# Constant matmuls in four of TensorE's waits, in the last two steps of a token loop

## Chip, cores and metric

The kernel runs on one core of one Trainium2 chip. The metric is the device time of one execution in microseconds (us). Engines are named as in the profile: PE is TensorE's matmul side, PEld its weight loads, DVE is VectorE, ACT is ScalarE, POOL is GpSimd, SP is SyncE.

## What is computed

The input x is 32 sequences of 64 tokens with 256 features, 2048 tokens in all. The reference, cut to its outline (every product in float32, except where the fake quantisation rounds):

```python
moe  = two_of_eight_experts(x, cond)              # three layers per expert, relu
x1   = x + tanh(softmax(causal(q k^T)) v @ Wo + bo)   # q, k, v = tanh(moe @ W + b), 16 heads of 64
a    = field_attention(x1, cond) @ Wout.T + bout      # 16 heads of 16, a coherence gate and a field term
x_q  = mxfp4_pseudo_quant(a, delta_act)           # blocks of 32 features
out  = x1 + x_q @ w_q.T + bias
```

## The kernel before

The kernel has three stages. A setup stage routes the tokens; an expert stage runs 39 slot tiles of 128 tokens; the last stage, called the token loop here, takes the 2048 tokens in TT = 16 tiles of 128. Each engine has its own program, written out by hand in the order in which it is to run, and semaphores tie the programs together. There is no scheduler: what stands later in an engine's program runs later on that engine.

The token loop is a software pipeline, `for t in range(0, TT + 3)`, so steps 0 to 18. In step t PE works on the first attention of tile t (names beginning `l1_`), finishes that of tile t-1, works on the second attention of tile t-2 (`l2_`), and on the last product of tile t-3 (`l2_turn_q`, `l2_ffn`). Every function first asks whether its tile exists and returns at once if not. So in steps 17 and 18 most of PE's program falls away:

- Step 17 (t = TT+1) has for PE the hidden layer and keys of tile 15 (L749, L737), its coherence gate (L758) and scores (`l2_scores`, L783), its values (`l2_v`, L768), then for tile 14 the transpose of the quantised rows (`l2_turn_q`, L823) and the last product (`l2_ffn`, L832), and then for tile 15 eight transposes (`l2_turn_p`, L685), the context (`l2_context`, L805) and the output projection (`l2_out`, L815).
- Step 18 (t = TT+2) has only `l2_turn_q` (L823) and `l2_ffn` (L832) of tile 15.

These wait for DVE or ACT. `l2_v` waits for the shifted scores (DVE L1398), because its result goes where the scores stood. `l2_turn_q` waits for the rounded rows (DVE L1079 to L1099), `l2_ffn` for the copy by ACT (L1044), `l2_turn_p` for the shares (DVE L1420). DVE then adds the field to the transposed shares (L1429, one for each half, the first as soon as four of the eight transposes are there), and PE's context (L805) waits for the second. After the context come the copy by ACT (L1038), the projection (L815), and on DVE the bias (L1436) and the blockwise rounding (L1079 to L1099). The last DVE instruction of a tile is `l2_result` (L1456), and SP stores what it wrote. A DVE program is strictly in order too: in step 17 `l2_result` of tile 14 stands between `l2_share` (L1420) and the first field addition of tile 15.

The waits of three of these functions in PE's program:

```python
def l2_v(t):       pe.wait_ge(u2_set, 2 * t + 2)
def l2_turn_q(t):  pe.wait_ge(xq_set, t + 1)
def l2_turn_p(t, n):                       # n == 0 / n == 1
    pe.wait_ge(p2_set, t + 1)  /  pe.wait_ge(fin_set, t)
```

PSUM bank 0 is used by the first attention only, whose last tile is read out in step 16. `ident_h` is a 128x128 identity matrix in bf16, held in the buffer `before` (the profile shows that name) since the expert stage. The f32 matmuls show twice as many instructions in the trace as the program has, the bf16 ones as many.

Of the kernel before, what the change touches and what calls it, by code (L numbers as in the profile page):

```python
# [26 lines left out]
P = 128  # L27
BATCH, SEQ, HID, COND = 32, 64, 256, 64
TOK = BATCH * SEQ
TT = TOK // P  # L30
# [46 lines left out]
def exists(t, n):  # L77

    return not isinstance(t, int) or 0 <= t < n
# [19 lines left out]
def build(nc, t_in, out):  # L99
    ctx = ExitStack()  # L100
    with ctx:
# [25 lines left out]
        ident_h = before  # L127
# [124 lines left out]
        bank = lambda b, n=512, parts=P: ps[0:parts, b, 0:n]  # L252
# [231 lines left out]
        def _(pe):  # L484
            mm = pe.matmul
# [4 lines left out]
            for k in range(KH):  # L490
                for g in range(4):
                    mm(ps[g * GATE_PAD:(g + 1) * GATE_PAD, 0, :], gate_w[:, k, :], x_t[:, k, g * 512:(g + 1) * 512],
                       start=k == 0, stop=False, tile_position=(0, g * GATE_PAD))
            pe.wait_ge(aug_loaded, 16)
            for g in range(4):
                mm(ps[g * GATE_PAD:(g + 1) * GATE_PAD, 1, :], gg_w,
                   part("cond", AUG_K)[:, g * 8:(g + 1) * 8].unsqueeze(2).to_broadcast([AUG_K, 8, SEQ]),
                   start=True, stop=True, tile_position=(0, g * GATE_PAD))
            for k in range(KH):
                pe.wait_ge(squared, k + 1)  # L500
                for g in range(4):
                    last = mm(ps[g * GATE_PAD:(g + 1) * GATE_PAD, 0, :], ones_w, sq_t[:, k, g * 512:(g + 1) * 512],
                              start=False, stop=k == KH - 1, tile_position=(0, g * GATE_PAD))
# [3 lines left out]
            for b, src in ((2, gate_t), (3, cond_t)):  # L507
                for n in range(4):
                    last = pe.transpose(ps[:, b, n * P:(n + 1) * P], src[:, n * P:(n + 1) * P], ident[:, :])
# [3 lines left out]
            for k in range(KH):  # L513
                last = mm(ps[:, 4, k * BATCH:(k + 1) * BATCH], part("we1", COND + 1)[:, k * P:(k + 1) * P],
                          part("cond", COND + 1), start=True, stop=True)
            for k in range(KH):
                last = mm(ps[:, 4, (KH + k) * BATCH:(KH + k + 1) * BATCH], part("wc1", AUG_K)[:, k * P:(k + 1) * P],
                          part("cond", AUG_K), start=True, stop=True)
# [7 lines left out]
            for n in range(TOPK * TT):  # L526
                last = mm(bank(0, 2 * SLOT_TILES), lo_hot[:, n, :], hi_ids[:, n, :, :], start=n == 0, stop=n == TOPK * TT - 1)
# [5 lines left out]
            for k in range(KH):  # L533
                last = mm(ps[0:BATCH, 7, 0:HID], f_hid[:, k, :], we2[:, k, :], start=k == 0, stop=k == KH - 1)
# [86 lines left out]
            def halves():  # L621

                return [(s, slice(s * SEQ, (s + 1) * SEQ)) for s in range(2)]

            def l1_turn_m(t):
                if not exists(t, TT):
                    return
                pe.wait_ge(m_set, t + 1)
                if t:
                    pe.wait_ge(exp1_set, 2 * t)  # L630
                for k in range(KH):
                    last = pe.transpose(ps[:, 0, k * P:(k + 1) * P], m_rows[:, k * P:(k + 1) * P], ident[:, :])
                last.then_inc(mt_ps, 1)

            def l1_project(t, wt, n):
                b = (3, 0)[n]
                for c in range(4):
                    f = (n * 4 + c) * P
                    for k in range(KH):
                        last = mm(ps[:, b, c * P:(c + 1) * P], wt[:, k, f:f + P], m_t[:, k, :],  # L640
                                  start=k == 0, stop=k == KH - 1)
                last.then_inc(qk_ps, 1)

            def l1_q(t, n):
                if not exists(t, TT):
                    return
                if n == 0:
                    pe.wait_ge(mt_set, t + 1)
                l1_project(t, wq, n)

            def l1_k(t, n):
                if not exists(t, TT):
                    return
                pe.wait_ge(qk_set, 4 * t + n + 1)
                l1_project(t, wk, n)

            def l1_v(t, s):
                if not exists(t, TT):
                    return
                pe.wait_ge(qk_set, 4 * t + 3 + s)  # L660
                for k in range(KH):
                    for r in range(2):
                        last = mm(ps[r * SEQ:(r + 1) * SEQ, (3, 0)[s], :], m_t[:, k, s * SEQ:(s + 1) * SEQ],  # L663
                                  wv[:, k, r * 512:(r + 1) * 512], start=k == 0, stop=k == KH - 1,
                                  tile_position=(0, r * SEQ))
                last.then_inc(v_ps, 1)
# [61 lines left out]
            def l2_q_or_k(t, b, wt):  # L728
                if not exists(t, TT):
                    return  # L730
                if t == 0:
                    pe.wait_ge(l2w_loaded, 16 * 5)
                if wt is wq2:
                    pe.wait_ge(x1t_set, t + 1)
                for c in range(C2):
                    for k in range(KH):
                        last = mm(ps[:, b, c * P:(c + 1) * P], wt[:, k, c * P:(c + 1) * P], x1_t[:, k, :],  # L737
                                  start=k == 0, stop=k == KH - 1)
                last.then_inc(qk2_ps, 1)

            def l2_hidden(t):
                if not exists(t, TT):
                    return
                if t:
                    pe.wait_ge(a_set, t)
                for c in range(KH):
                    dst = ps[:, 6, c * P:(c + 1) * P]
                    for k in range(KH):
                        last = mm(dst, wc1[:, k, c * P:(c + 1) * P], x1_t[:, k, :], start=k == 0, stop=k == KH - 1)  # L749
                last.then_inc(hc_ps, 1)  # L750
# [10 lines left out]
            def l2_v(t):  # L761
                if not exists(t, TT):
                    return
                pe.wait_ge(u2_set, 2 * t + 2)
                for s, q in halves():
                    for k in range(KH):
                        for r in range(2):
                            last = mm(ps[r * SEQ:(r + 1) * SEQ, 6, s * P:(s + 1) * P], x1_t[:, k, q],  # L768
                                      wv2[:, k, r * P:(r + 1) * P], start=k == 0, stop=k == KH - 1,
                                      tile_position=(0, r * SEQ))  # L770
                last.then_inc(v2_ps, 1)

            def l2_scores(t):
                if not exists(t, TT):
                    return
                pe.wait_ge(qk2_set, 2 * t + 2)
                for odd in range(2):
                    for r in range(2):
                        for g in range(4):
                            rows_ = slice(g * PAIR, (g + 1) * PAIR)  # L780
                            at = (2 * odd + r) * SEQ
                            for s, q in halves():
                                last = mm(ps[q, 4 + g, at:at + SEQ], q2_t[rows_, r, q], k2_t[rows_, odd * C2 + r, q],  # L783
                                          start=True, stop=True, tile_position=(g * PAIR, s * SEQ))
                last.then_inc(s2_ps, 1)
# [32 lines left out]
            def l2_turn_q(t):  # L818
                if not exists(t, TT):
                    return  # L820
                pe.wait_ge(xq_set, t + 1)
                for k in range(KH):
                    last = pe.transpose(turned_q[:, k, :], xq[:, k * P:(k + 1) * P], ident_h[:, :])  # L823
                last.then_inc(xqt_ps, 1)

            def l2_ffn(t):
                if not exists(t, TT):
                    return
                pe.wait_ge(xqt_set, t + 1)
                for k in range(KH):  # L830
                    for n in range(PARTS):
                        last = mm(bank(7, HID), xq_t[:, k, :], wffn[:, k, n, :], start=k + n == 0,  # L832
                                  stop=(k, n) == (KH - 1, PARTS - 1))
                last.then_inc(f_ps, 1)

            for t in range(0, TT + 3):
                l1_turn_m(t)
                l2_hidden(t - 2)
                l2_q_or_k(t - 2, 5, wk2)
                l1_q(t, 0)  # L840
                l2_coherence(t - 2)
                l2_scores(t - 2)
                l1_q(t, 1)
                l1_turn_p(t - 1, 0)
                l1_k(t, 0)
                l1_turn_p(t - 1, 1)
                l1_k(t, 1)
                l2_v(t - 2)
                l2_turn_q(t - 3)
                l1_context(t - 1)  # L850
                l2_ffn(t - 3)
                l1_v(t, 0)
                l2_turn_p(t - 2, 0)
                l1_v(t, 1)
                l2_turn_p(t - 2, 1)
                l1_out(t - 1)
                l2_context(t - 2)
                l1_scores(t)
                l1_turn_x1(t - 1)
                l2_out(t - 2)  # L860
                l2_q_or_k(t - 1, 4, wq2)
# [694 lines left out]
```

## Time and profile before

| quantity | value |
|---|---|
| time, median of 3 runs | 827.72 us |
| lowest and highest | 827.57 us, 828.91 us |
| profiled execution, its own time | 826.9 us |
| profiled execution, span | 825.1 us |
| mean granted clock of PE, as a share of full | 0.953 |
| PE busy | 747.6 us, 91% of the span |
| DVE busy | 496.2 us, 60% |
| ACT busy | 280.5 us, 34% |

The span is the part of the execution that the trace covers, and 1.8 us of the profiled execution lie outside it. All durations of instructions come from this one execution. PEclk is the clock that PE was granted: 1.00 stands for 2.4 GHz and 0.50 for 1.2 GHz. A PE row's duration runs from its first start to its last end, so a group of pipelined matmuls is shorter than their number times the duration of one.

### The profile page before, as it was taken

How to read it: one execution, taken by the hardware profiler on the slowest of the kernel's cores; microseconds unless marked ns; L12 is line 12 of the kernel's file. 1: busy time of each engine (PE TensorE's matmuls, PEld its weight loads, DVE VectorE, ACT ScalarE, POOL GpSimd, SP SyncE). 2: the span in 40 equal slices, each digit the busy share in tenths (PEclk: the TensorE clock that was granted, in tenths of full speed). 3: DMA queues.
4: the chain of work that ended last, by engine and by line, in shares of the span. 5: the costliest groups of instructions: out<-in, count | busy, mean ns of one | idle time of the engine just before them, and what ended most of it. 6: DMA issues, size and time to landing. Idle time of an engine off the chain costs nothing.

```text
span 825.1 us, 22545 instructions
## 1 busy us (share of the span) xinstructions
PE 747.6 (91%) x9214; PEld 647.6 (78%) x9214; DVE 496.2 (60%) x1081; ACT 280.5 (34%) x838; POOL 79.2 (10%) x90
## 2 busy tenths in 40 slices
PE   3169999999999999579999999999999999999774
PEld 1159989999999999457887789778987788778662
DVE  1845484444444444213677787778777877778765
ACT  4022212222112221023653355445643465346420
POOL 1031101111111100110000000000000000000000
PEclk9579999999999999888999999999999999999995
DMA  9677425111111100310000000000000000000000
GB/s 310 243 248 238 141 75 196 39 40 34 39 33 40 40 27 21 133 45 7 16 22 27 21 14 22 28 27 12 18 28 28 21 9 27 28 8 15 9 8 14
DMA packets 29668, 48.50 MB, mean 59 GB/s; under 512 B 3291, under 2 KB 19419, under 8 KB 29053
## 3 DMA queue, kind: packets, MB, share of 16 engines
q1 hardware_dynamic: 20493, 32.61, 11.8%
q0 software_dynamic: 3408, 9.31, 3.9%
q10 hardware_dynamic: 5664, 5.12, 1.8%
q8 instruction: 74, 1.21, 0.6%
q14 instruction: 29, 0.24, 0.1%
HBM read 39.82 MB, written 7.22 MB: 57 GB/s over the span
## 4 chain that ended last, share of the span: by engine, by line
PE 86%; DVE 8%; DMA 3%; issue 2%; ACT 1%; DVEq 0%; POOL 0%; SPq 0%; ACTq 0%; POOLq 0%
PE ps L566 17%; PE ps L640 15%; PE ps L555 8%; PE ps L578 8%; PE ps L663 7%; PE ps L717 7%; PE ps L685 4%; PE ps L737 3%; PE ps L678 2%; PE ps L708 2%; PE ps L768 2%; PE ps L815 2%; PE ps L749 2%; PE ps L783 2%; PE ps L805 1%
## 5 line engine op out<-in xcount | busy, mean ns | idle before, releaser
L566 PE MATMUL ps<-h_t,w_now 128*128 128x128 f32 x1248 | 146.0, 275 | 1.9 <-DVE h_t L1219 1.2
L566 PEld LDWEIGHTS ps<-h_t,w_now 128*128 128x128 f32 x1248 | 142.4, 192 | 2.8 <-issue 2.7
L640 PE MATMUL ps<-arena,l_weights 128*128 128x128 f32 x1024 | 130.2, 283 | 1.0 <-ACT arena L943 1.0
L640 PEld LDWEIGHTS ps<-arena,l_weights 128*128 128x128 f32 x1024 | 123.4, 198 | 2.7 <-ACT arena L943 1.8
L908 ACT ACTIVATE h_t<-ps,cols 128x128 f32<-128x128 f32 x156 | 44.5, 366 | 216.6 <-PE ps L555 195.0
L1210 DVE COPY w_now<-arena 128x2048 f32 x39 | 47.9, 1227 | 108.4 <-PE ps L566 100.3
L555 PEld LDWEIGHTS ps<-xg_t,w_now 128*128 128x128 f32 x624 | 76.8, 195 | 4.9 <-issue 2.6
L555 PE MATMUL ps<-xg_t,w_now 128*128 128x128 f32 x624 | 77.9, 279 | 2.3 <-issue 1.4
L949 ACT ACTIVATE arena<-ps,cols 128x128 f32<-128x128 f32 x256 | 72.8, 369 | 14.6 <-PE ps L640 14.6
L578 PE MATMUL ps<-arena,h_t 128*128 x312 | 73.9, 380 | 0.8 <-DVE y L1228 0.8
L465 POOL DMA_INDIRECT xg<-in_x,slot_tok x39 | 45.7, 1171 | 243.9 <-PE ps L545 204.2
L478 POOL DMA_INDIRECT arena<-expert_out,slot_of x32 | 30.2, 945 | 338.9 <-DVE arena L1312 330.2
L578 PEld LDWEIGHTS ps<-arena,h_t 128*128 128x128 f32 x312 | 56.3, 190 | 7.3 <-issue 1.2
L663 PE MATMUL ps<-l_weights,arena 128*64 128x512 f32 x256 | 61.5, 604 | 0.0
L717 PE MATMUL ps<-l_weights,arena 128*128 128x256 f32 x256 | 58.1, 380 | 0.0
L983 ACT ACTIVATE arena<-arena 128x256 f32<-128x256 f32 x16 | 6.7, 416 | 146.4 <-DVE arena L1350 146.4
L717 PEld LDWEIGHTS ps<-l_weights,arena 128*128 128x128 f32 x256 | 47.4, 190 | 6.8 <-DVE arena L1343 1.0
L1202 DVE COPY w_now<-arena 128x1024 f32 x39 | 27.1, 694 | 39.7 <-PE ps L555 33.4
L685 PEld LDWEIGHTS ps<-ident,arena 128*128 128x128 f32 x256 | 29.1, 144 | 26.0 <-issue 22.7
L1219 DVE TENSOR_SCALAR h_t<-ps,cols 128x128 f32<-128x128 f32 x156 | 43.7, 343 | 3.8 <-PE ps L566 3.8
L685 PE MATMUL ps<-ident,arena 128*128 128x128 f32 x256 | 41.0, 284 | 1.9 <-DVE arena L1420 1.2
L1318 DVE TENSOR_TENSOR arena<-ps,half_rows 128x512 f32<-128x512 f32 x32 | 22.0, 687 | 25.9 <-PE ps L663 25.9
(232 smaller groups left out, 977.9 us busy)
## 6 DMA issues: line engine op xcount, KB each, us to landing
arena<-in_w SPq DMA_DIRECT2D x16, 512.0 KB
arena<-in_w SPq DMA_DIRECT2D x8, 1024.0 KB
expert_out<-y ACTq DMA_DIRECT2D x39, 128.0 KB
arena<-in_x_t SPq DMA_DIRECT2D x1, 2048.0 KB, 8.1
arena<-in_x SPq DMA_DIRECT2D x16, 128.0 KB
out<-arena SPq DMA_DIRECT2D x16, 128.0 KB, 1.7
b<-in_b SPq DMA_DIRECT2D x1, 1024.0 KB, 12.7
l_weights<-in_wq SPq DMA_DIRECT2D x1, 1024.0 KB
```

The lines of the kernel that those rows point to most:

```text
L465: pool.indirect_dma_start(out=xg[j % XG][:, :], out_offset=None, in_=t_in["x"], in_offset=bass.IndirectOffsetOnAxis(ap=slot_tok[:, j:j + 1 ...
L555: last = mm(ps[:, 0, m * P:(m + 1) * P], w1_now[:, k, m * P:(m + 1) * P], xg_t[:, k, :], start=k == 0, stop=k == KH - 1)
L566: last = mm(ps[:, 2, m * P:(m + 1) * P], w2_now[:, k, m * P:(m + 1) * P], h1_t[j % 2][:, k, :], start=k == 0, stop=k == KM - 1)
L578: last = mm(bank(4, HID), h2_t[j % 2][:, k, :], flat[:, bass.ds(at + k * HID, HID)], start=k == 0, stop=k == KM - 1)
L640: last = mm(ps[:, b, c * P:(c + 1) * P], wt[:, k, f:f + P], m_t[:, k, :], start=k == 0, stop=k == KH - 1)
L663: last = mm(ps[r * SEQ:(r + 1) * SEQ, (3, 0)[s], :], m_t[:, k, s * SEQ:(s + 1) * SEQ], wv[:, k, r * 512:(r + 1) * 512], start=k == 0, stop ...
L685: last = pe.transpose(bank_[:, m * P:(m + 1) * P], p[:, h:h + 2, :], ident[:, :])
L717: last = mm(bank(1, HID), ctx_t[:, c, :], wo[:, c, :], start=c == 0, stop=c == C1 - 1)
L908: last = f(h1_t[j % 2][:, k, :], ps[:, 0, k * P:(k + 1) * P], ACT.Relu, bias=cols[:, bass.ds(e * KM + at + k, 1)])
L949: last = f(dst[:, cc, :], ps[:, (3, 0)[n], c * P:(c + 1) * P], ACT.Tanh, bias=col(bias)[:, cc:cc + 1])
L1210: dve.tensor_copy(w2_now[:, :, :].rearrange("p k n -> p (k n)"), arena[:, bass.ds(at, KM * MID)]).then_inc(w2_set, 1)
L1219: last = ts(h2_t[j % 2][:, k, :], ps[:, 2, k * P:(k + 1) * P], cols[:, bass.ds(e * KM + at + k, 1)], 0.0, ALU.add, ALU.max)
```

## The change

A helper `tail_busy` issues n matmuls of the bf16 identity with itself, 128 columns each, into bank 0, in one step only. None of them waits for a semaphore and none signals one; nothing reads what they write. It is called in four places: 84 ahead of everything in step 18; in step 17, 44 between `l2_scores` and `l2_v`, 12 between `l2_v` and `l2_turn_q`, and 26 between `l2_ffn` and `l2_turn_p`. No other engine's program changes.

```diff
+            def tail_busy(t, last, n):
+                if t == last:
+                    for _ in range(n):
+                        mm(bank(0, P), ident_h[:, :], ident_h[:, :], start=True, stop=True)
+
             for t in range(0, TT + 3):
+                tail_busy(t, TT + 2, 84)
                 l1_turn_m(t)
                 l2_hidden(t - 2)
                 l2_q_or_k(t - 2, 5, wk2)
                 l1_q(t, 0)
                 l2_coherence(t - 2)
                 l2_scores(t - 2)
+                tail_busy(t, TT + 1, 44)
                 l1_q(t, 1)
...
                 l2_v(t - 2)
+                tail_busy(t, TT + 1, 12)
                 l2_turn_q(t - 3)
                 l1_context(t - 1)
                 l2_ffn(t - 3)
+                tail_busy(t, TT + 1, 26)
                 l1_v(t, 0)
                 l2_turn_p(t - 2, 0)
```

The end of PE's program before, from what follows the scores of tile 15 (L783) in step 17 to the last product (L832) in step 18:

```order
L768 MATMUL ps<-arena 64x128 x8
L823 MATMUL ps<-before,arena 128x128 x2
L832 MATMUL ps<-wffn,arena 128x256 x6
L685 MATMUL ps<-ident,arena 128x128 x8
L805 MATMUL ps<-arena 32x64 x32
L815 MATMUL ps<-arena 128x256 x2
L823 MATMUL ps<-before,arena 128x128 x2
L832 MATMUL ps<-wffn,arena 128x256 x6
```

The same stretch with the change, where L839 is the matmul in the helper:

```order
L839 MATMUL ps<-before 128x128 x44
L768 MATMUL ps<-arena 64x128 x8
L839 MATMUL ps<-before 128x128 x12
L823 MATMUL ps<-before,arena 128x128 x2
L832 MATMUL ps<-wffn,arena 128x256 x6
L839 MATMUL ps<-before 128x128 x26
L685 MATMUL ps<-ident,arena 128x128 x8
L805 MATMUL ps<-arena 32x64 x32
L815 MATMUL ps<-arena 128x256 x2
L839 MATMUL ps<-before 128x128 x84
L823 MATMUL ps<-before,arena 128x128 x2
L832 MATMUL ps<-wffn,arena 128x256 x6
```

No instruction has changed places with another; 166 matmuls now stand in front of four waiting ones.

## Rows read from the trace of the kernel before

**Rows 1.** The page: PE's granted clock in 40 equal slices, in tenths

```profile
PEclk9579999999999999888999999999999999999995
```

**Rows 2.** The page: shares of the chain that ended last, by engine

```profile
PE 86%; DVE 8%; DMA 3%; issue 2%; ACT 1%; DVEq 0%; POOL 0%; SPq 0%; ACTq 0%; POOLq 0%
```

**Rows 3.** Stretches: bounds, length, PE busy (instructions), granted clock, DMA share, GB/s

```profile
38.00:40.00 2.00, 1.25 (x20) 0.50 0.00 0
368.40:372.40 4.00, 1.75 (x65) 1.00 0.23 66
373.50:379.20 5.70, 5.69 (x26) 0.50 0.01 3
774.50:778.50 4.00, 2.26 (x73) 1.00 0.02 4
778.00:782.00 4.00, 1.09 (x16) 1.00 0.01 2
795.00:799.00 4.00, 3.03 (x83) 1.00 0.00 0
799.20:802.40 3.20, 0.00 (x0) 1.00 0.02 5
802.50:805.80 3.30, 2.36 (x18) 0.50 0.00 0
```

**Rows 4.** Timeline, step 17: start, length, engine, line, operation, count, idle before and releaser

```profile
802.65 1.97 PE L768 MATMUL ps<-arena 128*64 128x128 f32 x16 [3.48 <-DVE arena L1398]
...
805.41 0.40 PE L823 MATMUL ps<-before,arena 128*128 128x128 bf16 x2 [0.78 <-DVE arena L1099]
...
806.27 1.46 PE L832 MATMUL ps<-wffn,arena 128*128 128x256 bf16 x6 [0.46 <-ACT arena L1044]
...
808.89 1.97 PE L685 MATMUL ps<-ident,arena 128*128 128x128 f32 x8 [1.16 <-DVE arena L1420]
...
810.05 0.69 DVE L1429 TENSOR_TENSOR arena<-ps,arena 128x512 f32<-128x512 f32 x1 [0.81 <-PE ps L685]
...
810.90 0.69 DVE L1429 TENSOR_TENSOR arena<-ps,arena 128x512 f32<-128x512 f32 x1 [0.16 <-PE ps L685]
...
811.65 1.18 PE L805 MATMUL ps<-arena 64*32 64x64 f32 x64 [0.78 <-DVE arena L1429]
...
813.29 2.08 PE L815 MATMUL ps<-arena 128*128 128x256 f32 x4 [0.46 <-ACT arena L1038]
```

**Rows 5.** Timeline, step 18

```profile
820.07 0.39 PE L823 MATMUL ps<-before,arena 128*128 128x128 bf16 x2 [4.71 <-DVE arena L1099]
...
820.93 1.46 PE L832 MATMUL ps<-wffn,arena 128*128 128x256 bf16 x6 [0.46 <-ACT arena L1044]
...
822.43 0.48 DVE L1456 SCALAR_TENSOR_TENSOR arena<-ps,act_inv,arena 128x256 f32<-128x256 f32 x1 [2.42 <-PE ps L832]
```

**Rows 6.** Timeline, step 16

```profile
785.95 0.66 PE L685 MATMUL ps<-ident,arena 128*128 128x128 f32 x4
...
787.40 1.28 DVE L1429 TENSOR_TENSOR arena<-ps,arena 128x512 f32<-128x512 f32 x2
...
791.19 0.86 PE L805 MATMUL ps<-arena 64*32 64x64 f32 x64
...
792.96 1.03 PE L815 MATMUL ps<-arena 128*128 128x256 f32 x4
```

**Rows 7.** Timeline, step 15

```profile
757.46 0.28 PE L823 MATMUL ps<-before,arena 128*128 128x128 bf16 x2
...
758.77 0.83 PE L832 MATMUL ps<-wffn,arena 128*128 128x256 bf16 x6
```

**Rows 8.** Lines L815, L832, L527: ns min/median/max, first and last start us

```profile
L815 PE MATMUL ps<-arena x64: 379/379/796, 420.4 to 814.7; 128*128 128x256 f32 x64
L832 PE MATMUL ps<-wffn,arena x96: 272/273/421, 436.0 to 822.0; 128*128 128x256 bf16 x96
L527 PE MATMUL ps<-arena x32: 246/263/267, 38.7 to 40.7; 128*128 128x78 bf16 x32
```

## The prediction

> **What bounds the kernel now.** I read the page first. Its chain of work that ended last runs for 86% over PE, with 8% on DVE [rows 2], so for most of the span only less PE work would help. The change adds PE work, and it sits where PE waits, in the last 27 us. There the second thing on the page matters: PE's granted clock stands at or near full through nearly the whole second half and falls in the last slice [rows 1]. The stretches put a place to it. From 799.20 to 802.40 us PE does nothing, still at 1.00; from 802.50 it is granted 0.50 [rows 3], and every later PE row of steps 17 and 18 is a slow one. The timeline shows which. The first four idle gaps that the change fills are the waits ahead of L768 (3.48 us), L823 (0.78 us), L685 (1.16 us) [rows 4] and, the longest, L823 in step 18 (4.71 us) [rows 5]. None of them is PE's own fault: DVE works through its chain (L1398; L1099; L1420; L1099 again).
>
> So the last 25 us alternate between DVE's chain, which PE's clock doesn't touch, and short PE bursts at 1.2 GHz that DVE or ACT then waits for. Which bursts lie on the path? In step 17, L768, L823 and L832 don't. L768 ends at 804.62 and L823 starts only at 805.41, held by DVE; L832 ends at 807.73, and DVE, in order, reaches its consumer L1456 only after the shares L1420, on which L685 waits until 808.89. From L685 on, everything is in series: the transposes, the field additions L1429 (idle ahead of both: 0.81 and 0.16 us, on PE), the context L805, a copy by ACT, the projection L815 [rows 4], the rounding on DVE, L823, a copy by ACT, L832 and the last DVE instruction [rows 5].
>
> **What the change adds and what it is worth.** It removes nothing. 44 + 12 + 26 + 84 = 166 bf16 matmuls of 128 columns are added, each with a weight load of 128 columns, in front of four waiting functions. They can pay only through the clock: if PE is no longer idle ahead of 802.5 us, it may keep 2.4 GHz to the end. The same instructions at full clock stand in the steps before.
>
> First the gain, burst by burst, on the path only.
>
> - Transposes and field additions. At half clock L685 starts at 808.89 and the second L1429 ends at 810.90 + 0.69 = 811.59 [rows 4]. At full clock four transposes take 0.66 us, and the two additions back to back 1.28 us [rows 6]. With 0.05 us of hand-over they end at 808.89 + 0.66 + 0.05 + 1.28 = 810.88. Gain 0.71 us.
> - L805: 1.18 us [rows 4] against 0.86 us [rows 6]. Gain 0.32 us.
> - L815: 2.08 us [rows 4] against 1.03 us [rows 6]. Gain 1.05 us.
> - L823 in step 18: 0.39 us [rows 5] against 0.28 us [rows 7]. Gain 0.11 us.
> - L832 in step 18: 1.46 us [rows 5] against 0.83 us [rows 7]. Gain 0.63 us.
>
> Sum: 0.71 + 0.32 + 1.05 + 0.11 + 0.63 = 2.82 us. ACT's copies and DVE's instructions are counted at no change.
>
> Now the cost. The added matmuls cost nothing while they end before the wait would have ended; after that every one delays what stands behind it. So the price of one is what matters. The trace has no stream of just this form. Nearest at full clock: L832, bf16 and 256 columns, six in 0.83 us [rows 7] with 273 ns for one [rows 8], so (0.83 - 0.273) / 5 = 111 ns from start to start, and 56 ns for half the columns. That takes the weight load as hidden. From the other side: L527 has the same full bf16 weight load with only 78 columns, 32 of them from 38.7 to 40.7 us [rows 8], at a granted clock of 0.50 [rows 3]. That is 2.0 / 31 = 65 ns each, no more than 78 columns at 1.2 GHz take; so such a load fits into 65 ns even there. The price lies between 56 and 65 ns, and I take 57, by L832, which it resembles in everything but the columns.
>
> - 84 in step 18. The cover is DVE's rounding. At full clock the four instructions of L815 end after 1.03 us, 379 ns each [rows 8], so they start (1.03 - 0.379) / 3 = 0.217 us apart, and the first added matmul can start 4 x 0.217 = 0.87 us after L815's start. L823 waits until 1.03 + 4.71 = 5.74 us after it. That leaves 4.87 us, or 58.0 ns for each of 84. At 57 ns they take 4.79 and cost nothing; at 65 ns 5.46, 0.59 us late. Late here is late at the end, one for one, because L823 and L832 are the end.
> - 26 in step 17, between L832 and L685. L832 starts at 806.27, its six take 0.67, the 26 another 1.48: done at 808.42, under DVE's L1420 until 808.89. At 65 ns 808.63, still covered.
> - 12 ahead of L823. L768 starts at 802.65 and at full clock takes about half of its 1.97 us, 1.0; the 12 take 0.7 more and end at about 804.3, before 805.41.
> - 44 ahead of L768: 3.48 us wait, 2.5 us at 57 ns, 2.9 at 65.
>
> At 1.2 GHz, L832 takes (1.46 - 0.421) / 5 = 208 ns from start to start [rows 5, 8], and 128 columns at 1.2 GHz are 107 ns; then 26 take 2.8 us, and 84 take 9.0 us. So the fillers are free at full clock and dear at half clock. That is where a loss could come from.
>
> Here a rule of the Trainium skill speaks against the change. "TensorE: Matmul & The Clock Gate", section "Back-to-back issue gap", says that a stream of weight load and matmul pairs with 128 columns runs at about 81 ns per matmul, not at the 56 ns of an isolated gap. An estimate by that page: 84 x 81 ns = 6.8 us, 1.9 us over the cover, 26 some 0.2 us over, and the gain falls to 0.7 us. L527's 65 ns at the lower clock are against it, so I don't take the 81.
>
> **The sum.** Against its own execution: 826.9 - 2.8 = 824.1 us. The median of the runs shown is 0.8 us above that execution, so 827.7 - 2.8 = **824.9 us**, 0.34% faster. A measurement of this kernel can tell about 0.2%, 1.65 us, from no change.
>
> **The rivals.**
>
> 1. *As above, full clock to the end, fillers under their cover* (chance 0.60). For it: the stretch 795 to 799 us with 3.03 us of PE work in 4 was at 1.00 and stayed so [rows 3], and the 44 carry such a density on to 801.7. Own range 824.3 to 825.6.
> 2. *The weight loads bind at full clock* (0.08). A load that doesn't get faster with the clock would make the price up to L527's 65 ns. Then the 84 end 0.6 us late: 825.5. The page's 81 ns is the stronger form of this.
> 3. *The clock still falls, once, in step 17, and comes back before L815* (0.14). After the 44 there remains 1.0 us of idle, after the 12 another 1.1 us. In 802.6 to 806.6 PE would work about 0.9 + 0.7 + 0.3 + 0.3 = 2.2 us of 4. PE stayed at 1.00 after 2.26 us of 4 (774.5 to 778.5) and fell after 1.75 of 4 (368.4 to 372.4) and after 1.09 of 4 (778 to 782) [rows 3]; 2.2 is near the one that stayed, and not far from the other. If it falls at about 806, L832 at half clock ends its columns at 806.27 + 1.28 = 807.55 and 26 at 107 ns end at 810.33, 1.4 us after 808.89. Against that, such a dense stretch brings the clock back: 373.5 to 379.2, solid PE work at 0.50, was followed by 1.00 within 5.7 us. Net gain between 2.8 - 0.9 (back in the middle of the 26) and 2.8 - 1.4 - 0.7 - 0.3 = 0.4 (back at L815). 825.8 to 827.3, half of it on either side of the bound.
> 4. *The change doesn't do what it says* (0.08). The clock falls at another phase of the program in most executions, the fillers don't count as work for it or come too late, yet the cover hides them. 827.0 to 828.0.
> 5. *Slower: the 84 start at half clock* (0.10). One mechanism: PE has fallen to 1.2 GHz by L815 and wakes up only inside the 84. With up to 5.7 us of solid work at 0.50 before the rise [rows 3], 53 of them take 5.7 us and 31 take 1.8, together 7.5 us against 4.9 of cover: 2.6 us late. If the 26 ran at half clock too, 1.4 more. Of the gain only L823 and L832 in step 18 remain, 0.7 us. 827.7 + 2.6 + 1.4 - 0.7 = 831.0; with a rise after 3.5 us it is 33 at half clock and 51 at full, 6.4 us, 1.5 late, 829.9. It decides as soon as the clock is low where L815 ends. For it: the clock in step 17 has been low at just that place. Against it: 44 + 12 + 26 fillers lie before it.
>
> **How the numbers follow.** Faster by over 0.2%, that is below 826.1: rivals 1 and 2 and half of 3, less a little for noise: 0.73. Within 0.2%: the rest of 3, and 4: 0.17. Slower: 0.10, from 5. The predicted time is that of case 1. For the range I leave out 0.10 above, case 5, and some 0.06 of case 3 and 4, and about 0.04 below: 824.0 to 827.4.
>
> **What the changed profile would show.** Granted clock at 1.00 from about 785 us to the end; no idle stretch of over 1.3 us on PE after 799; L815 at 1.03 us and L832 in step 18 at 0.83; 84 rows of L839 in 4.7 to 4.9 us, with the wait ahead of L823 in step 18 still ending on DVE L1099. It would be wrong if that wait ended on nothing but the queue in front (price above 58 ns), if 0.50 stood anywhere after 799, or if L685's start moved off DVE's L1420.

## The result, and the profile after

The change made the kernel faster by about what was forecast, and the time still fell outside the range. Over 17 runs each, 823.66 us (821.87 to 826.82) stand against 826.37 us (824.49 to 828.91) before: a ratio of 0.9967, 95% interval 0.9956 to 0.9979. That is 2.7 us, where 2.8 were forecast. But the forecast was 824.9 us with a range from 824.0, because it stood on three runs of before with a median of 827.72, and the 17 have one of 826.37.

The page of the changed kernel, PE's granted clock in 40 slices, is to be held against [rows 1]:

```profile
PEclk9579999999999999878999999999999999999989
```

The last slice is no longer a 5. The stretches of steps 17 and 18 (bounds, length, PE busy with instructions, granted clock, DMA share, GB/s) answer to the last two of [rows 3]:

```profile
799.20:802.40 3.20, 3.20 (x107) 1.00 0.03 5
802.50:805.80 3.30, 2.03 (x31) 1.00 0.00 0
805.80:809.30 3.50, 2.50 (x34) 1.00 0.02 5
809.30:812.70 3.40, 2.00 (x74) 1.00 0.11 39
812.70:816.10 3.40, 2.94 (x41) 1.00 0.02 5
816.10:822.00 5.90, 4.02 (x60) 1.00 0.00 1
```

The stretch in which PE did nothing is full, and the clock stays at 1.00. PE's timeline over the same steps, with L839 the added matmuls, answers to [rows 4, 5]:

```profile
799.18 0.91 PE L783 MATMUL ps<-arena 32*64 32x64 f32 x64 [0.86 <-ACT arena L1015]
800.03 2.63 PE L839 MATMUL ps<-before 128*128 128x128 bf16 x44
803.58 1.09 PE L768 MATMUL ps<-arena 128*64 128x128 f32 x16 [0.92 <-DVE arena L1407]
804.60 0.84 PE L839 MATMUL ps<-before 128*128 128x128 bf16 x12
806.34 0.28 PE L823 MATMUL ps<-before,arena 128*128 128x128 bf16 x2 [0.89 <-DVE arena L1108]
807.09 0.83 PE L832 MATMUL ps<-wffn,arena 128*128 128x256 bf16 x6 [0.47 <-ACT arena L1053]
807.75 1.61 PE L839 MATMUL ps<-before 128*128 128x128 bf16 x26
809.83 1.09 PE L685 MATMUL ps<-ident,arena 128*128 128x128 f32 x8 [0.46 <-DVE arena L1429]
811.86 0.86 PE L805 MATMUL ps<-arena 64*32 64x64 f32 x64 [0.94 <-DVE arena L1438]
813.18 1.13 PE L815 MATMUL ps<-arena 128*128 128x256 f32 x4 [0.46 <-ACT arena L1047]
814.15 4.85 PE L839 MATMUL ps<-before 128*128 128x128 bf16 x84
819.02 0.29 PE L823 MATMUL ps<-before,arena 128*128 128x128 bf16 x2
819.77 0.83 PE L832 MATMUL ps<-wffn,arena 128*128 128x256 bf16 x6 [0.47 <-ACT arena L1053]
```

Three of the four waits still end on DVE, 0.92, 0.89 and 0.46 us after the fillers. Only the L823 of step 18, the last row but one, has no wait any more: the 84 end at 819.00, and DVE's rounding, whose last row is

```profile
818.54 0.42 DVE L1108 TENSOR_TENSOR arena<-arena 128x256 bf16<-128x256 f32 x1
```

ends at 818.96. In step 17 L823 started 0.06 us after the end of DVE's last rounding row (806.28 to 806.34); by the same distance it would have started at 819.02 here, which is when it did.

One measure serves for all that follows, since executions of one kernel differ by 2 us and more in what lies before it: the **tail**, from the start of step 17's scores (L783) to the end of the span. Before, L783 began at 798.26 us of 825.1, a tail of 26.8 us. Now it is 823.3 - 799.18 = 24.1 us. The two profiled spans differ by 1.8 us only, because the changed kernel had reached L783 0.9 us later. 0.7 us of that lies in step 16: its clock, which had fallen before too, was low longer, and from L823 to L805 it took 9.4 us instead of 8.7. That is no effect of the change that a run shows: it lies ahead of every added matmul, and among the eleven profiles without fillers in step 16 the same stretch takes anything from 8.7 to 9.4 us.

### The profile page after: what moved, and what is told of

Its sections match the earlier page's. It is cut to its first block, busy times and chain, and to the rows that moved or that the text cites. A ratio compares the mean times of both kernels' runs of the same rounds, so it can differ in the third digit from the quotient of the medians.

```text
span 823.3 us, 22877 instructions
## 1 busy us (share of the span) xinstructions
PE 753.3 (92%) x9380; PEld 655.1 (80%) x9380; DVE 496.3 (60%) x1081; ACT 281.6 (34%) x838; POOL 79.2 (10%) x90
## 4 chain that ended last, share of the span: by engine, by line
PE 87%; DVE 7%; DMA 3%; issue 1%; ACT 1%; DVEq 0%; POOL 0%; SPq 0%; ACTq 0%; POOLq 0%
PE ps L566 17%; PE ps L640 15%; PE ps L555 8%; PE ps L578 8%; PE ps L663 7%; PE ps L717 7%; PE ps L685 4%; PE ps L737 3%; PE ps L708 2%; PE ps L678 2%; PE ps L768 2%; PE ps L749 2%; PE ps L815 2%; PE ps L783 2%; PE ps L832 1%; PE ps L805 1%
## 5 line engine op out<-in xcount | busy, mean ns | idle before, releaser
L640 PE MATMUL ps<-arena,l_weights 128*128 128x128 f32 x1024 | 130.0, 282 | 1.0 <-ACT arena L952 1.0
L640 PEld LDWEIGHTS ps<-arena,l_weights 128*128 128x128 f32 x1024 | 123.2, 198 | 2.7 <-ACT arena L952 1.8
L578 PE MATMUL ps<-arena,h_t 128*128 x312 | 73.9, 380 | 0.8 <-DVE y L1237 0.8
L578 PEld LDWEIGHTS ps<-arena,h_t 128*128 128x128 f32 x312 | 56.3, 190 | 7.3 <-issue 1.2
L663 PE MATMUL ps<-l_weights,arena 128*64 128x512 f32 x256 | 61.5, 604 | 0.0
L717 PE MATMUL ps<-l_weights,arena 128*128 128x256 f32 x256 | 58.5, 382 | 0.0
L717 PEld LDWEIGHTS ps<-l_weights,arena 128*128 128x128 f32 x256 | 47.8, 192 | 6.7 <-DVE arena L1352 0.8
L685 PEld LDWEIGHTS ps<-ident,arena 128*128 128x128 f32 x256 | 28.9, 143 | 24.6 <-issue 22.7
L685 PE MATMUL ps<-ident,arena 128*128 128x128 f32 x256 | 40.8, 284 | 0.8 <-DVE arena L1429 0.5
```

The costliest lines, as they stand in the source:

```text
L578: last = mm(bank(4, HID), h2_t[j % 2][:, k, :], flat[:, bass.ds(at + k * HID, HID)], start=k == 0, stop=k == KM - 1)
L685: last = pe.transpose(bank_[:, m * P:(m + 1) * P], p[:, h:h + 2, :], ident[:, :])
L717: last = mm(bank(1, HID), ctx_t[:, c, :], wo[:, c, :], start=c == 0, stop=c == C1 - 1)
```

## The experiments

All fillers are the bf16 matmuls of the change unless said otherwise. Tails are worked out from the start of L783 and the span of each profile, and each ratio is to runs of before on the same chip as the run. At 0.1 to 0.4% the ratios often can't separate two neighbours in the table, so the readings below rest on the tails: the nine profiles with the change's tail lie between 24.06 and 24.14 us.

| run | fillers | tail | ratio to before, 95% interval |
|---|---|---|---|
| before | none | 26.8 | |
| the change | 44, 12, 26, 84 | 24.1 | 0.9967 (0.9956 to 0.9979) |
| the change, run again | the same | 24.1 | 0.9974 (0.9962 to 0.9986) |
| without 84 | 44, 12, 26 | 24.8 | 0.9972 (0.9960 to 0.9984) |
| only 84 | 84 | 27.3 | 1.0004 (0.9996 to 1.0013) |
| 44 and 84 | 44, 84 | 27.3 | 1.0002 (0.9989 to 1.0015) |
| without 12 | 44, 26, 84 | 24.1 | 0.9989 (0.9975 to 1.0003) |
| 124 for 84 | 44, 12, 26, 124 | 26.1 | 1.0002 (0.9992 to 1.0012) |
| transposes | 44, 12, 26, 84 | 24.1 | 0.9963 (0.9950 to 0.9976) |
| step 16 too | + 24, 24 | 24.1 | 0.9956 (0.9943 to 0.9969) |
| loop's start too | + 170, 12, 20 | 24.1 | 0.9965 (0.9952 to 0.9978) |
| setup too | + 160, 60 | 24.1 | 0.9969 (0.9958 to 0.9981) |
| whole token loop | + 24, 24, 195, 12, 20 | 24.1 | 0.9939 (0.9924 to 0.9955) |
| loop and setup | the last + 200, 70, 20 | 24.1 | 0.9925 (0.9906 to 0.9945) |

### Without the 84

```diff
-                tail_busy(t, TT + 2, 84)
```

> The 84 matmuls of step 18 are left out; 44, 12 and 26 stay. Theory (the fillers pay through PE's clock alone, each group by keeping it up for the bursts behind it): 1.00 until after L815, which takes 1.03 to 1.13 us, then PE idles for 4.7 us, the clock falls as it fell in the 3.3 us of idleness of step 17 before, and L823 and L832 of step 18 take 0.39 and 1.46 us. Gain against before 2.8 - 0.7 = 2.1 us, ratio 0.9975. Rival 1 (the gain of the change has little to do with the clock, or the clock would stay up through that wait anyway): L832 at 0.83 us and the whole 2.8 us, ratio 0.9967. Rival 2 (the 84 are what brings the clock back, the others do nothing): no gain, ratio 1.000.

The timeline of the end of this kernel:

```profile
811.01 1.13 PE L815 MATMUL ps<-arena 128*128 128x256 f32 x4 [0.46 <-ACT arena L1046]
816.86 0.39 PE L823 MATMUL ps<-before,arena 128*128 128x128 bf16 x2 [4.71 <-DVE arena L1107]
817.71 1.46 PE L832 MATMUL ps<-wffn,arena 128*128 128x256 bf16 x6 [0.46 <-ACT arena L1052]
```

L815 is fast, then PE idles for 4.71 us, and L823 and L832 are back at their half-clock times, to the hundredth those of [rows 5]. The tail is 821.8 - 797.02 = 24.8 us, 0.7 longer than that of the change. So the three groups of step 17 carry 2.1 us of the gain and the 84 carry 0.7, as expected. Both rivals fall: the first by L832's 1.46 us in the trace (the ratio alone would allow it), the second by the ratio too.

### Only the 84

```diff
-                tail_busy(t, TT + 1, 44)
-                tail_busy(t, TT + 1, 12)
-                tail_busy(t, TT + 1, 26)
```

> Only the 84 matmuls of step 18; 44, 12 and 26 are left out. Theory: the clock falls at about 802 us as before and is at 0.50 when L815 ends; 84 start at 107 ns each, the clock rises after 3.5 to 5.7 us of them, and they end 1.5 to 2.6 us after DVE's L1099 would have let L823 go; L823 and L832 then run at full clock (0.7 us less). Net 0.8 to 1.9 us slower than before, ratio 1.001 to 1.002. This is the mechanism of the forecast's fifth case. Rival: the clock rises at once or the wait still covers them, and they gain 0.7 us, ratio 0.999.

The timeline, and under it the stretches on both sides of the rise:

```profile
810.65 2.08 PE L815 MATMUL ps<-arena 128*128 128x256 f32 x4 [0.47 <-ACT arena L1044]
812.52 6.35 PE L839 MATMUL ps<-before 128*128 128x128 bf16 x84
818.70 0.28 PE L823 MATMUL ps<-before,arena 128*128 128x128 bf16 x2
819.44 0.83 PE L832 MATMUL ps<-wffn,arena 128*128 128x256 bf16 x6 [0.46 <-ACT arena L1050]
```

```profile
812.50:815.40 2.90, 2.90 (x29) 0.50 0.00 0
815.50:822.00 6.50, 4.31 (x66) 0.99 0.05 17
```

Up to L815 step 17 is that of before again, 17.12 us from L783's start to L815's end against 17.11. The 84 begin at half clock, and after some 3 us the clock is at full. They take 6.35 us instead of 4.85. L823 starts 18.70 - (10.65 + 2.08) = 5.97 us after L815's end instead of 4.71, so it is 1.26 us late, and 0.74 us come back from L823 and L832: +0.5 us in the tail. That is a little under the 0.8 that was the lower end of the expectation, because the clock rose sooner than the 3.5 us taken for it. The same 84 matmuls that are free behind fillers cost half a microsecond in the tail without them; the whole time can't tell that from nothing (1.0004, 0.9996 to 1.0013). The mechanism of the forecast's fifth case exists.

### Without 12 and 26, and without 12

```diff
-                tail_busy(t, TT + 1, 12)
-                tail_busy(t, TT + 1, 26)
```

> 44 and 84 stay, 12 and 26 are left out. In steps 17 and 18, from the start of L783 to the span's end, before took 26.8 us, the change 24.1. Theory (all three groups of step 17 are needed): without 12 and 26 PE works only about 1.1 + 0.3 + 0.8 us between L768 and L685, a stretch of 6.2 us, so the clock falls there, L685, L805 and L815 run at 0.50, and the 84 start slow and end 1.5 us late: 25.5 to 27.3 us. Rival (only the longest wait of step 17 mattered, 12 and 26 are decoration): 24.1 us with 1.00 throughout.

PE's timeline of it in step 17 and the stretches:

```profile
805.58 0.28 PE L823 MATMUL ps<-before,arena 128*128 128x128 bf16 x2 [1.66 <-DVE arena L1106]
806.33 0.83 PE L832 MATMUL ps<-wffn,arena 128*128 128x256 bf16 x6 [0.46 <-ACT arena L1051]
809.07 1.97 PE L685 MATMUL ps<-ident,arena 128*128 128x128 f32 x8 [1.91 <-DVE arena L1427]
```

```profile
804.00:807.80 3.80, 1.11 (x8) 1.00 0.00 0
807.90:818.10 10.20, 7.78 (x102) 0.51 0.05 14
```

L832 still runs at full clock, L685 no longer. The clock fell at about 808.1 us: in the 3.8 us shown PE had worked 1.11 us, and the wait of 1.91 us ahead of L685 had lasted only 0.9 us. Everything to L815 is at half clock, the 84 take 6.28 us, and the tail is 825.7 - 798.43 = 27.3 us: all that the 44 had won is lost again. The theory holds, and the ratio, 1.0002 (0.9989 to 1.0015), lies clear of the change's.

The second run took out the 12 alone.

> 44, 26 and 84 stay, only the 12 between L768 and L823 in step 17 are left out. With 12 and 26 both left out the clock fell between L832 and L685. Theory (26 alone carry that place, 12 are decoration): 1.00 throughout and 24.1 us from L783's start to the end, as the change. Rival (PE's work between 803.6 and 807 us, 1.1 + 0.3 us in some 3.5, is too little without the 12): a fall at about 805 to 808 us, L832 and the 26 at half clock, 25 to 28 us.

In its profile the clock stayed up and the tail is 822.6 - 798.49 = 24.1 us, which is the theory's figure. But its times don't agree with a free omission: 8 of 12 lie between 823.3 and 825.0 us, the other 4 from 825.3 to 829.0, and the ratio is 0.9989 beside 0.9974 for the change on the same chip. The profiled execution was one of the 8. The granted clock averaged over each run is on record. It is 0.966 and 0.967 in two of those four and 0.963 in the other two, where the change has 0.960 to 0.969 and the run without 12 and 26 has 0.954 to 0.960. So a fall as in that run doesn't explain at least two of the four. Whether the 12 are needed stays open; that the 26 are needed where the 12 are missing is what the two runs show together.

### 124 in place of 84

```diff
-                tail_busy(t, TT + 2, 84)
+                tail_busy(t, TT + 2, 124)
```

> 124 matmuls instead of 84 in step 18, all else as changed. Theory: the 84 fill DVE's rounding to within 0.1 us, so the 40 more are late one for one, 40 x 56 ns = 2.2 us, with the clock at 1.00: L839's group of step 18 takes 7.0 to 7.1 us, and the time is 2.2 us above that of the change, 0.5 us under before, ratio 0.9994. Rival (a price of 65 ns from weight loads that bind): 2.6 us and more, ratio 1.000.

```profile
811.82 7.09 PE L839 MATMUL ps<-before 128*128 128x128 bf16 x124
818.74 0.28 PE L823 MATMUL ps<-before,arena 128*128 128x128 bf16 x2
```

40 more matmuls take 7.09 - 4.85 = 2.24 us, 56.0 ns each, a weight load for each included. The tail is 823.0 - 796.86 = 26.1 us, 2.0 above the change: 40 x 56 ns less 0.2 us of cover that the 84 had left. The 65 ns and the 81 ns of the forecast are both out at full clock, for this filler. The ratio, 1.0002, is a little above the 0.9994 expected, within the interval.

### Transposes as fillers

```diff
+            turned_0 = ps[:, 0, 0:P // 2].bitcast(BF16)
-                        mm(bank(0, P), ident_h[:, :], ident_h[:, :], start=True, stop=True)
+                        pe.transpose(turned_0, ident_h[:, :], ident_h[:, :])
```

> The same 44, 12, 26 and 84 places and numbers, but each filler is a transpose of the bf16 identity (by a matmul with the identity, bf16 result) in place of a plain matmul. Theory (any stream of array work keeps the clock): as the change, ratio 0.9967, clock 1.00 to the end. Rival, the Trainium skill, TensorE: Matmul & The Clock Gate, Part 4: PE-mode transpose, which says that full clock does not engage for transposes: the clock falls at about 802 us in spite of the 44, everything behind runs at 0.50, the 84 take 9 us, and the time is some 4 to 7 us above before, ratio 1.005 to 1.008.

```profile
797.89 2.63 PE L841 MATMUL ps<-before 128*128 128x128 bf16 x44
812.00 4.85 PE L841 MATMUL ps<-before 128*128 128x128 bf16 x84
```

They take the same time as matmuls and keep the clock as well: tail 821.1 - 797.04 = 24.1 us, ratio 0.9963. The Trainium skill (TensorE: Matmul & The Clock Gate, Part 4: PE-mode transpose) says that full clock does not engage for transposes; it stayed at 1.00 over these 24 us.

### Step 16

```diff
+                tail_busy(t, TT, 24)
                 l2_v(t - 2)
+                tail_busy(t, TT, 24)
                 tail_busy(t, TT + 1, 12)
```

> The change, with 24 more matmuls ahead of L768 and 24 ahead of L823 in step 16, where PE waits 1.76 and 1.67 us and the clock falls for 3.4 us in the profile of before and for 6.8 us in that of the change. Theory: 1.00 through step 16; L708 takes 1.16 us instead of 1.99, L832 0.83 instead of 1.46; most of it lies beside DVE's chain, so 0 to 0.9 us less than the change (0.9 where the slow stretch reached L717 and L685). Rival: the clock falls all the same, or the fillers delay L768 and L823; 0 to 0.5 us more.

```profile
782.98 1.16 PE L708 MATMUL ps<-arena 64*64 64x64 f32 x64
784.07 0.83 PE L832 MATMUL ps<-wffn,arena 128*128 128x256 bf16 x6
786.25 0.66 PE L685 MATMUL ps<-ident,arena 128*128 128x128 f32 x4 [1.35 <-DVE arena L1431]
```

L708 and L832 are at full clock and end 1.35 us sooner than DVE lets L685 go. From step 16's L823 to its L805 this kernel takes 8.7 us, as before did with its 3.4 us at half clock. So a short fall there costs nothing, because DVE covers it, and the 6.8 us of the changed kernel's profile, which reached L685 and L717, cost 0.7. Even that is the most that any profile shows: the changed kernel run again had a low clock over L685 too and took 8.7 us. The theory holds; the whole time (0.9956) can't tell it from the change.

### The start of the token loop, and the setup

In the profiles of before and of the change the clock is also low in other places, and there the burst behind the wait is long and PE is the bound.

```diff
+            def early_busy(t, at, n):
+                if t == at:
+                    for _ in range(n):
+                        mm(bank(7, P), ident_h[:, :], ident_h[:, :], start=True, stop=True)
             for t in range(0, TT + 3):
                 tail_busy(t, TT + 2, 84)
+                early_busy(t, 0, 170)
+                early_busy(t, 1, 20)
...
+                early_busy(t, 0, 12)
                 l1_scores(t)
```

> The change, with 170 matmuls ahead of step 0 of the token loop (PE waits 11.4 us there), 12 ahead of the scores of step 0 and 20 ahead of step 1 (waits of 0.8 and 1.3 us). In both profiles the clock is low over the first 3.5 us of the 9.1 us of L640 in step 0, and for 3.4 to 6.8 us in step 1, and there PE is the bound. Theory (what stands on solid PE work at half clock comes back in full): 1.8 us in step 0 and 1.2 to 2.9 us in step 1, together 3.0 to 4.6 us below the change. Rival (instruction supply or DMA, not the clock, is short there: the scores of step 0 show idle gaps put down to issue): under 1 us.

From the first L632 (start of step 0) to the second burst of L663 (in step 1), before takes 385.52 - 353.97 = 31.6 us, the change 31.3, this kernel 28.1: 3.2 us less than the change, inside what was expected. Step 1 was now at full clock. Step 0 was not: the 170 ended 1.7 us before L632, and L640 still took 8.81 us. The median, 823.19 us of 5 runs, shows none of this gain.

Two things make the 3.2 us too large. First, this stretch varies by itself: in the eleven profiles that have no fillers here it takes 28.9 to 31.6 us, with a median of 30.5, and those of before and of the change are at the slow end. Second, its start moved. L632 waits for DVE, and DVE for the gathered rows. From the end of the last L578 to L632 it is 10.8 to 11.7 us in the eleven profiles and 12.04 in this one:

```profile
352.80 0.35 DVE L1328 TENSOR_SCALAR arena<-arena,weight_of 128x256 f32<-128x256 f32 x1 [10.54 <-DMA arena<-expert_out,slot_of]
353.73 0.44 PE L632 MATMUL ps<-ident,arena 128*128 128x128 f32 x2 [1.67 <-DVE arena L1329]
```

DVE's wait for the rows is 9.2 to 10.1 us in the eleven. From the start of the last L578 to the second L663, which takes in both, the eleven have a median of 43.5 us (42.3 to 45.0) and this kernel 42.2. So what the profile shows is about 1.3 us, less than was expected. Why the rows came later is not shown.

The setup had fillers in a run of its own:

```diff
+            for _ in range(160):
+                mm(bank(7, P), before[:, :], before[:, :], start=True, stop=True)
             pe.wait_ge(hot_set, 1)
...
             pe.wait_ge(ids_set, 1)
+            for _ in range(60):
+                mm(bank(1, P), before[:, :], before[:, :], start=True, stop=True)
```

> The change, with 160 matmuls ahead of L527 in the setup (PE waits 13.4 us) and 60 ahead of the first transposes of the expert stage (4.3 us of wait), operand the triangular bf16 matrix that the buffer holds then. Theory: L527's 32 take 1.2 us instead of 2.0 to 2.3, the first expert layer (L555, 16 matmuls) 1.8 us instead of 3.5: 1.0 + 1.7 = 2.7 us below the change, if the clock is up when they start. Rival (the 160 or the 60 run at 107 ns and end late): 0 to 3 us above the change.

It gained nothing (ratio 0.9969). The 160 ended 3.06 us too early, and the burst that they were meant for was slow as before. The 60 ended 1.01 us ahead of two transposes (L548), which ran fast, but 2.72 us ahead of the first expert layer (L558), and that was slow too:

```profile
25.47 10.57 PE L526 MATMUL ps<-before 128*128 128x128 bf16 x160
39.10 2.26 PE L530 MATMUL ps<-arena 128*128 128x78 bf16 x32 [3.06 <-DVE arena L1187]
42.70 3.78 PE L617 MATMUL ps<-before 128*128 128x128 bf16 x60
47.49 0.44 PE L548 MATMUL ps<-ident,xg 128*128 128x128 f32 x2 [1.01 <-issue]
49.20 3.57 PE L558 MATMUL ps<-xg_t,w_now 128*128 128x128 f32 x16 [1.27 <-ACT xg_t L913]
```

So the last runs let the fillers reach up to the burst: 195 in place of 170 in the loop, and 200, 70 and another 20 (ahead of the first expert layer) in the setup. First the loop alone, with step 16:

> The change with all fillers of the token loop tried so far: 24 and 24 in step 16, and 195 (170 had left 1.7 us of idleness, in which the clock fell), 12 and 20 at its start. Theory: clock 1.00 from the first expert steps to the end; against the change 1.7 us less in step 0 (the 3.4 us at half clock under L640), 1.2 to 2.9 less in step 1, 0 to 0.9 less in step 16: 3 to 5 us below the change, ratio to before 0.991 to 0.993. Rival (the wait ahead of step 0 varies with its transfers, so 195 either end late or too early to hold the clock): no better than the change plus 1.2 us, ratio 0.995.

```profile
356.16 0.44 PE L632 MATMUL ps<-ident,arena 128*128 128x128 f32 x2 [0.68 <-DVE arena L1331]
357.14 7.41 PE L640 MATMUL ps<-arena,l_weights 128*128 128x128 f32 x64 [0.54 <-ACT arena L962]
```

L640 takes 7.41 us where before took 9.10, and from L632 to the second L663 it is 383.00 - 356.16 = 26.8 us, 4.5 below the change. But here too L632 comes late, 12.44 us after the end of the last L578. From the start of the last L578 it is 383.00 - 341.73 = 41.3 us, 2.2 below the median of the eleven profiles. Median 821.45 us, ratio 0.9939: some 5 us under before and 2.6 under the change run again beside it (824.06). That is a little short of the 3 to 5 us expected, and it fits the 2.2 us with the 0 to 0.7 of step 16. Then with the setup:

> The former with fillers in the setup too: 200 ahead of L527 (160 ended 3.1 us early and the clock fell there), 70 ahead of the first transposes of the expert stage and 20 ahead of its first layer. Theory: L527 1.2 us instead of 2.3, the first layer 1.8 instead of 3.5, 2.7 us below the former, ratio 0.988 to 0.990. Rival (the setup's end is set by the gathers and DVE's copies, not by PE's bursts): under 1 us, or later by what the 200 and 70 overrun.

Its page, and the two bursts of the setup:

```profile
PEclk9899999999999999999999999999999999999999
```

```profile
38.88 1.35 PE L530 MATMUL ps<-arena 128*128 128x78 bf16 x32 [0.94 <-DVE arena L1199]
48.36 2.00 PE L560 MATMUL ps<-xg_t,w_now 128*128 128x128 f32 x16
```

From the product with the mask (L522) to the second expert layer's start, before takes 30.7 us and this kernel 29.0, so 1.7 us of the 2.7 expected came. 819.74 us (818.02 to 822.08, 6 runs), ratio 0.9925 (0.9906 to 0.9945): some 6 us under before, and the fastest kernel of this study. Its interval and that of the kernel with the loop's fillers alone overlap; the profile is what separates them. The 200 began at a granted clock of 0.50 and had it at 1.00 2.8 us later, well inside their 12.67 us, so a start at half clock is no harm under a wait that long. And in step 16 of this profile the clock fell at about 772.2 us, after a stretch from 768.20 to 772.20 us with 2.88 us of PE work. The first 24 fillers stand behind that, begin at half clock and take 2.58 us instead of 1.50, so the fillers of step 16 can come too late to hold it:

```profile
772.42 1.11 PE L692 MATMUL ps<-ident,arena 128*128 128x128 f32 x4 [0.19 <-DVE arena L1397]
773.33 2.58 PE L846 MATMUL ps<-before 128*128 128x128 bf16 x24
```

The changed kernel was run once more for these:

> The changed kernel itself, on the chip of the three others, to have the same-chip distance: 2.7 us below before (ratio 0.9967), 24.1 us from L783's start to the end.

It gave 824.06 us against 826.60, ratio 0.9974, tail 819.7 - 795.60 = 24.1 us.

## Why the prediction was right in its mechanism and wrong in its range

- **The step that failed** is the level that the gain was taken from: "The median of the runs shown is 0.8 us above that execution, so 827.7 - 2.8 =" 824.9 us. The range hung on it, "and about 0.04 below: 824.0". Three runs within 1.4 us of each other were taken for the level, and the profiled execution's 824.1 us was passed over for the median's 824.9. The 17 runs of before span 824.49 to 828.91 us with a median 1.35 below, and beside the experiments before had medians of 825.39, 826.63 and 826.60. 0.9 us of room below the forecast was for the gain's own error and had nothing for that level. As a ratio the forecast was 824.9 / 827.72 = 0.9966, and 0.9967 was measured. That the two agree to 0.0001 is in part luck, since the interval is 0.9956 to 0.9979; what supports the mechanism is the tail, term by term.
- **The terms of the sum.** Transposes and field additions: from 809.83 to the end of the second L1429 (now L1438), one DVE row of 1.29 us from 810.52, is 1.98 us against 2.70, gain 0.72 (forecast 0.71). L805 gave 0.32 (0.32), L832 0.63 (0.63), L823 0.10 (0.11). L815 gave 0.95, not 1.05: at this place it takes 1.13 us in every run in which the clock stayed up, and 1.03 in step 16. Sum 2.72; the tail fell by 2.7.
- **The price of a filler.** "I take 57": 56.0 ns. "4.87 us" of cover for the 84, 0.17 to spare at 56 ns: the run with 124 found 0.2. The bursts off the path (L768, L823, L832 in step 17) ran faster and gave nothing, as said.
- **The signs.** Of what the changed profile was to show, three things came otherwise. The clock was back at 1.00 at about 789 us and not at 785, because of step 16. L815 took 1.13 us. And the wait ahead of L823 in step 18 had gone, which was named as the sign of a price above 58 ns, though the price was 56.0: the row of 84 ends at about the moment at which DVE lets L823 go.
- **The Trainium skill's 81 ns** (TensorE: Matmul & The Clock Gate, Back-to-back issue gap) would have made the gain 0.7 us by the forecast's estimate. The profile of a burst with the same weight load was right to be preferred, and 2.24 us for 40 settle it.
- **Case 3** (a fall in step 17 after all) did not come in the changed kernel's profiles. How near it is, the run without 12 and 26 shows, where the clock fell after 1.11 us of work in 3.8. The forecast judged the case by PE's work in 4 us, "2.2 is near the one that stayed", and that comparison is weaker than it looked: with all fillers, the clock fell in step 16 after 2.88 us of work in 4.
- **Case 5** (slower) is real as a mechanism, but dearer in the forecast (2.2 to 3.3 us above before) than in the run built for it (0.5), since the clock rose some 3 us into the 84 (3.5 and 5.7 had been taken), and since the 26 weren't there to be late.

## What to carry to other kernels

Ahead of a burst on the path, a wait of PE has a second price, the burst itself at half clock: look for rows of one line with two durations, and fill first the waits ahead of long bursts where PE is the bound (2.7 us in the last two steps here, about 2 in the loop's first two, nothing measurable in step 16). Independent matmuls held the clock here where they reached to within about 1 us of the next instruction (0.92, 0.89, 0.46 us in step 17; 1.04 us ahead of the loop with all fillers) and the long burst followed at once or after 0.5 us. They are free as long as they fit the wait, at 56 ns each at full clock and about 100 at half (29 of the 84 alone in 2.90 us). Ended 3.06 us ahead of the long burst, or 2.72 and 2.64 us with two short transposes between, they brought little or nothing for it (setup and loop start). Begun at half clock they cost time where the wait was 4.7 us (the 84), and did their work where it was 13.4 us (the 200). When a stretch of one profile is compared with that of another, take its start where nothing has changed yet, and look at how much it varies among the unchanged ones. And forecast a ratio, or give the level of before its own spread in the range.

## What the runs showed of the hardware

- A bf16 transpose into bf16 costs PE the same as a bf16 matmul of 128 columns (84 in 4.85 us each way) and kept the granted clock at 1.00 just as well.
- The clock fell after stretches that were far from idle: with PE busy 1.11 us of 3.8 (without 12 and 26), at the loop's start with 1.75 of 4 [rows 3], and with all fillers in step 16 with 2.88 of 4, while it stayed up after 2.26 of 4 at the same place of before [rows 3].
- After a wait of 4.71 us, and after one of 3.06, the next burst was wholly at half clock (L832 1.46 us; 32 matmuls of L530 2.26 us, against 1.35 at full).
